# Final stage of a graph-and-experts layer: the weighted sums moved to TensorE as diagonal products

## The reference, cut to what matters

```python
sel = take_along_axis(expert_out, topk_idx)          # two rows of 256 for each node
moe = sum(topk_w[..., None] * sel, axis=2)
y = x + moe                                          # x: the node's own normalised row
mu, var = mean(y), var(y)                            # over the 256 features
out = x_in + (y - mu) / sqrt(var + eps) * gamma + beta
```

## Time and profile before

| | |
|---|---|
| median of three runs | 1391.78 us |
| profiled execution: span from first to last instruction | 1391.8 us |
| mean granted TensorE clock over the span | 0.917 |
| TensorE last busy at | 1314.1 us |
| first load of the final stage issued at | 1317.41 us |
| last VectorE instruction ends at | 1387.63 us |

### The profile page before, as it was taken

One profiled execution on the slowest core, in us unless ns is written; L12 is line 12 of the kernel. 1 busy time (PEld: TensorE's weight loads), 2 busy tenths in 40 slices (PEclk: granted clock), 3 DMA queues, 4 the chain that ended last, 5 costly groups with the idle time before them and its releaser, 6 DMA issues.

```text
span 1391.8 us, 24409 instructions
## 1 busy us (share of the span) xinstructions
PE 1101.7 (79%) x6668; PEld 776.1 (56%) x6669; DVE 910.6 (65%) x2128; ACT 525.3 (38%) x1408; POOL 853.7 (61%) x968
## 2 busy tenths in 40 slices
PE   6799987999968878778887888888943999999700
PEld 4476543444446545545554555557842999999700
DVE  7599998999976666566665666633566333433276
ACT  3567655767713233333333233213420332332212
POOL 5362228999977777777777777750004577755326
PEclk9899998999979999999999999969965999999955
DMA  5000000000023333333333333357722122222392
GB/s 165 16 26 17 14 15 3 0 0 0 0 64 100 103 105 102 102 105 99 106 102 101 104 106 105 104 72 225 256 98 87 61 72 69 71 72 68 83 261 78
DMA packets 50239, 115.99 MB, mean 83 GB/s; under 512 B 11113, under 2 KB 24783, under 8 KB 50040
## 3 DMA queue, kind: packets, MB, share of 16 engines
q0 software_dynamic: 26832, 74.54, 18.6%
q1 hardware_dynamic: 23336, 40.64, 9.7%
HBM read 97.15 MB, written 17.99 MB: 83 GB/s over the span
## 4 chain that ended last, share of the span: by engine, by line
PE 44%; DVE 14%; DMA 14%; issue 13%; POOL 10%; ACT 2%; DVEq 2%; SPq 1%; POOLq 0%; ACTq 0%
PE bank L1813 10%; DMA big<-msg_rows,const 10%; PE bank L2063 8%; PE bank L2074 8%; POOL big L721 5%; POOL big L661 4%; DVE node_buf L1275 3%; PE bank L1757 2%; DVE big L1202 2%; PE bank L1977 2%; PE bank L1774 2%; PE bank L1683 1%; DVE big L1228 1%; DMA big<-xn_rows 1%; DMA x_buf<-x 1%
## 5 line engine op out<-in xcount | busy, mean ns | idle before, releaser
L721 POOL DMA_INDIRECT big<-msg_rows,const x416 | 407.1, 979 | 126.6 <-issue 80.6
L1813 PE MATMUL bank<-big 128*128 128x256 f32 x832 | 242.5, 417 | 88.2 <-DMA big<-msg_rows,const 53.6
L1275 DVE TENSOR_TENSOR node_buf<-node_buf,bank 125x256 f32 x416 | 173.6, 417 | 201.6 <-PE bank L1813 147.7
L1813 PEld LDWEIGHTS bank<-big 128*128 128x128 f32 x832 | 150.7, 201 | 154.2 <-DVE node_buf L1275 88.9
L1202 DVE TENSOR_SCALAR big<-bank,big 125x416 bf16<-125x416 f16 x400 | 183.7, 492 | 0.0
L966 ACT ACTIVATE big<-bank 128x500 f32<-128x500 f32 (+1 forms) x208 | 107.4, 572 | 179.8 <-PE bank L1865 179.8
L1060 ACT ACTIVATE mid<-bank,const 128x128 f32<-128x128 f32 x256 | 73.0, 368 | 207.9 <-PE bank L2063 207.9
L705 POOL TENSOR_TENSOR big<-big 125x512 f32<-125x512 f32 x125 | 142.1, 1172 | 10.6 <-PE bank L1757 9.3
L661 POOL TENSOR_TENSOR big<-big 125x256 f32<-125x256 f32 (+1 forms) x100 | 55.5, 555 | 112.7 <-ACT big L787 106.7
L2074 PE MATMUL bank<-big,mid 128*128 x512 | 121.0, 380 | 0.0
L1683 PE MATMUL bank<-big 125*128 125x416 bf16 x400 | 102.7, 348 | 21.2 <-DVE big L1202 10.2
(11 more groups left out here) (304 smaller groups left out, 2001.5 us busy)
## 6 DMA issues: line engine op xcount, KB each, us to landing
big<-L_ffn_w SPq DMA_DIRECT2D x32, 512.0 KB, 6.1
big<-msg_rows,const POOLq DMA_INDIRECT x416, 2.7
big<-moe_rows SPq DMA_DIRECT2D x10, 560.0 KB
msg_rows<-big SPq DMA_DIRECT2D x25, 125.0 KB
xn_rows<-mid POOLq DMA_DIRECT2D x5, 625.0 KB, 5.9
x_buf<-x SPq DMA_DIRECT2D x5, 560.0 KB
big<-xn_rows SPq DMA_DIRECT2D x5, 560.0 KB
out<-big SPq DMA_DIRECT2D x5, 560.0 KB
```

The costliest lines, as they stand in the source:

```text
L721: pool.indirect_dma_start(msgs[slot], None, msg_rows, bass.IndirectOffsetOnAxis(edge_idx[:, n:n + 1], 0)).then_inc(msgs_in[slot // 2], 16)
L1275: dve.tensor_tensor(rows, rows, agg_ps[2 * half + j][0:P, :], ALU.add).then_inc(s.agg_add, 1)
L1813: mm(agg_ps[k % 4], hot_src[:, turn, k, :], msgs[slot], start=True, stop=True, skip_group_check=True).then_inc(s.agg_mm, 1)
```

## The change

The two weighted sums leave VectorE. Each becomes a product on TensorE with a diagonal matrix: `diag0[t]` is 125 x 125 with the first weights of tile t on its diagonal, `diag1[t]` has the second weights. The own rows are multiplied with the identity, so that three products accumulate own + w0 * pick0 + w1 * pick1 in one PSUM bank (`bank[t % 8]`). VectorE takes the statistics from PSUM, and ScalarE normalises out of PSUM into `pick0`.

- ScalarE makes the diagonals `diag0` (an activation that scales the identity by a column of weights), those of groups 0 and 1 as soon as `y_ok` has reached 64, those of group g + 2 behind the normalising of group g.
- GpSimd makes `diag1` in the same rhythm, behind the `gamma` multiplications of group g, and does no residual additions any more.
- VectorE does all five residual additions of a group, and does those of group g - 1 between the statistics of group g and `shift_of(g)`.
- SP loads the own rows of group 0 when `y_ok` is 64, without waiting for the scatters, and those of group g + 1 behind the expert rows of group g.
- Tile t waits on TensorE for `fin_norm` of tile t - 8, whose bank it takes.

The diff, without the declarations of semaphores and buffers:

```diff
@@ sync engine: loads and stores
+            def load_rows(g, view, dram):
+                rows = slice(G * g, G * g + G)
+                for lo, hi in ((0, 112), (112, P)):
+                    sp.dma_start(view[lo:hi, rows, :], tiled(dram)[lo:hi, rows, :]).then_inc(fin_in[g], 16)
+
+            sp.wait_ge(s.y_ok, NT)
+            load_rows(0, own, xn2_rows)
             for k in range(2):
                 sp.wait_ge(y_out[k], 16 * (NT // 2))
             for g in range(T // G):
-                rows = slice(G * g, G * g + G)
-                for view, dram in ((pick0, moe_rows[0:N]), (pick1, moe_rows[N:2 * N]), (own, xn2_rows)):
-                    for lo, hi in ((0, 112), (112, P)):
-                        sp.dma_start(view[lo:hi, rows, :], tiled(dram)[lo:hi, rows, :]).then_inc(fin_in[g], 16)
+                load_rows(g, pick0, moe_rows[0:N])
+                load_rows(g, pick1, moe_rows[N:2 * N])
+                if g < T // G - 1:
+                    load_rows(g + 1, own, xn2_rows)
             for g in range(T // G):
                 rows = slice(G * g, G * g + G)
-                sp.wait_ge(s.fin_ok, (G - len(VECTOR_ADDS)) * (g + 1))
-                sp.wait_ge(s.fin_ok_too, len(VECTOR_ADDS) * (g + 1))
+                sp.wait_ge(s.fin_ok, G * (g + 1))
@@ GpSimd
-            pool.wait_ge(s.beta_ok, T)
-            for t in range(T):
-                pool.wait_ge(s.fin_norm, t + 1)
-                pool.tensor_tensor(pick0[:, t, :], pick0[:, t, :], gamma_bc, ALU.mult).then_inc(s.fin_gamma, 1)
-                if t % G not in VECTOR_ADDS:
-                    pool.wait_ge(s.fin_gamma, t + 1)
-                    pool.tensor_tensor(pick0[:, t, :], pick0[:, t, :], x_sb[:, t, :], ALU.add).then_inc(s.fin_ok, 1)
+            pool.wait_ge(s.y_ok, NT)
+
+            def second_diagonals(g):
+                for t in range(G * g, G * g + G):
+                    pool.tensor_scalar(diag1[:, t, :], ident[0:P, 0:P], weight[:, t, 1:2], None, ALU.mult).then_inc(s.diag1_ok, 1)
+
+            second_diagonals(0)
+            second_diagonals(1)
+            for g in range(T // G):
+                for t in range(G * g, G * g + G):
+                    pool.wait_ge(s.fin_norm, t + 1)
+                    pool.tensor_tensor(pick0[:, t, :], pick0[:, t, :], gamma_bc, ALU.mult).then_inc(s.fin_gamma, 1)
+                if g + 2 < T // G:
+                    second_diagonals(g + 2)
@@ ScalarE
+            def first_diagonals(g):
+                for t in range(G * g, G * g + G):
+                    act.activation(diag0[:, t, :], ident[0:P, 0:P], ACT.Copy, scale=weight[:, t, 0:1]).then_inc(s.diag0_ok, 1)
+
+            act.wait_ge(s.y_ok, NT)
+            first_diagonals(0)
+            first_diagonals(1)
             for g in range(T // G):
                 act.wait_ge(s.fin_stats, g + 1)
                 act.activation(rstd[:, g * G:g * G + G], mv[:, g * G:g * G + G, 1], ACT.Sqrt, bias=eps_t).then_inc(s.fin_root, 1)
                 act.wait_ge(s.fin_shift, g + 1)
                 for t in range(G * g, G * g + G):
-                    act.activation(pick0[:, t, :], pick1[:, t, :], ACT.Identity, scale=rstd[:, t:t + 1],
+                    act.activation(pick0[:, t, :], bank[t % 8][0:P, 0:D], ACT.Identity, scale=rstd[:, t:t + 1],
                                    bias=fin_shift[:, t:t + 1]).then_inc(s.fin_norm, 1)
+                if g + 2 < T // G:
+                    first_diagonals(g + 2)
@@ VectorE
             def residual(g):
-                for t in [G * g + j for j in VECTOR_ADDS]:
+                for t in range(G * g, G * g + G):
                     dve.wait_ge(s.fin_gamma, t + 1)
-                    dve.tensor_tensor(pick0[:, t, :], pick0[:, t, :], x_sb[:, t, :], ALU.add).then_inc(s.fin_ok_too, 1)
+                    dve.tensor_tensor(pick0[:, t, :], pick0[:, t, :], x_sb[:, t, :], ALU.add).then_inc(s.fin_ok, 1)
             for g in range(T // G):
                 tiles = range(G * g, G * g + G)
-                dve.wait_ge(fin_in[g], 6 * 16)
                 for t in tiles:
-                    last = dve.scalar_tensor_tensor(pick0[:, t, :], pick0[:, t, :], weight[:, t, 0:1], own[:, t, :], ALU.mult, ALU.add)
-                step(last)
-                for t in tiles:
-                    last = dve.scalar_tensor_tensor(pick1[:, t, :], pick1[:, t, :], weight[:, t, 1:2], pick0[:, t, :], ALU.mult, ALU.add)
-                step(last)
-                for t in tiles:
-                    last = dve.bn_stats(stats[:, t, :], pick1[:, t, :])
+                    dve.wait_ge(s.fin_mm, t + 1)
+                    last = dve.bn_stats(stats[:, t, :], bank[t % 8][0:P, 0:D])
                 step(last)
                 for t in tiles:
                     last = dve.bn_aggr(mv[:, t, :], stats[:, t, :])
                 last.then_inc(s.fin_stats, 1)
                 if g:
-                    shift_of(g - 1)
-                if g > 1:
-                    residual(g - 2)
-            shift_of(T // G - 1)
-            residual(T // G - 2)
+                    residual(g - 1)
+                shift_of(g)
             residual(T // G - 1)
@@ TensorE, behind the expert stage
+            pe.wait_ge(s.y_ok, NT)
+            for t in range(T):
+                if t % G == 0:
+                    pe.wait_ge(fin_in[t // G], 6 * 16)
+                if t >= 8:
+                    pe.wait_ge(s.fin_norm, t - 7)
+                total = bank[t % 8][0:P, 0:D]
+                mm(total, ident[0:P, 0:P], own[:, t, :], start=True, stop=False)
+                pe.wait_ge(s.diag0_ok, t + 1)
+                mm(total, diag0[:, t, :], pick0[:, t, :], start=False, stop=False)
+                pe.wait_ge(s.diag1_ok, t + 1)
+                mm(total, diag1[:, t, :], pick1[:, t, :], start=False, stop=True).then_inc(s.fin_mm, 1)
```

More of the change, by code:

```diff
@@ L39 @@
 BEHIND = [[], [], [0, 1], [2, 3], [4]]
-VECTOR_ADDS = (3, 4)
 MAGIC = 12582912.0
@@ L225, in __init__ @@
         self.fin_shift = sem("fin_shift")
+        self.diag0_ok = sem("diag0_ok")
+        self.diag1_ok = sem("diag1_ok")
+        self.fin_mm = sem("fin_mm")
         self.fin_ok = sem("fin_ok")
-        self.fin_ok_too = sem("fin_ok_too")
         self.stored = sem("stored")
@@ L362, in program @@
         own = m.take([T, D], parts=P)
+        diag0 = m.take([T, P], parts=P)
+        diag1 = m.take([T, P], parts=P)
         b = Region(big, 0, NX * 2048)
```

## The result

The changed kernel takes 1376.84 us, the median of four runs (1374.81 to 1378.89), beside 1392.39 for the kernel before (1391.77 to 1394.47, four runs). The ratio is 0.988, with a 95% interval from 0.9864 to 0.9897: 15.6 us less. The forecast was 1376.5, or 15.3 us less.

What follows compares the result with a forecast made beforehand. Loads bound the early groups, then VectorE, slowed beside GpSimd. Group 2's products end at 1347.6; loops of 7.6 us bring group 4's to 1362.8, and the tail of 13.7 gives 1376.5 us, range 1371 to 1387.

Steps and rivals of the forecast that it cites:

- The loads: Start of final stage: own rows of group 0 move while the last scatter lands, so each group lands 2.5 us earlier.
- the case of no gain: Low end for the loads: the early load delays the scatters as much, so the gain is nothing instead of 2.5 us.
- The half clock of group 0: TensorE starts group 0 at half clock: 5 us for two tiles, then 3.9 us for three, 8.9 us in all.
- The loop over the banks: Tile 3 waits for the bank of the previous group's tile 0: 5.0 us plus 2.6 for tiles 3 and 4, 7.6 a group.
- the waits at tile 3: Sign expected in the changed profile: TensorE's waits inside a group fall on the normalising, at tile 3.
- The tail: From group 4's last product to the end: 5.0, multiplications 4.0, last addition 0.5, and 4.2 to the end: 13.7 us.
- Contention: Final stage before: two-input VectorE work beside two-input GpSimd work takes 0.79 us an instruction, not 0.41; 10.65 us a group.
- the rival of no gain: VectorE and GpSimd stay at 10.65 us a group for another reason; kernel about 1390 us; chance 0.04.
- GpSimd's diagonals: Making diagonals on GpSimd: 0.28 to 0.60 us each, nearest 0.41; a GpSimd group of multiplications and diagonals 6.1 us.
- Statistics from PSUM: VectorE statistics read from PSUM: no difference taken from SBUF; 0.1 us either way a piece, at most 0.5 us a group.
- half-clock case: Rivals on TensorE: half clock throughout, 1402 us, chance 0.08; or at the start of every group, 1383 us, chance 0.10.
- Stores ahead of the loads: Rival: early stores make groups 3 and 4 land 2.5 and 5 us later; kernel 1379 to 1381 us; chance 0.10.

Runs made afterwards that it cites:

- first experiment: Changed kernel with group 0's own rows loaded behind the wait for the scatters, ahead of the expert rows: ratio to the kernel before 0.9909, 63.4 us of stage.
- third experiment: Changed kernel with 28 unused products on TensorE before the first landing to keep the clock up: ratio to the kernel before 0.9908, 63.2 us of stage.
- the quiet GpSimd: Kernel before, GpSimd silent in the final stage: gamma multiplications left out, all residual additions and the sums on VectorE; ratio 0.9891, 62.5 us of stage.

## Why the prediction was right, step by step

**The time** was right by luck in part, since errors cancelled. The forecast sum, counted into the stage, is 47.9 us to the last product and 13.7 to the end, 61.6. Measured: 49.5 and 12.3, 61.8. Behind the 49.5 is a second pair of errors: TensorE began 2.8 us later than forecast and took 0.5 us more for group 0, and then won back 1.7 us over groups 2 to 4, which took 21.1 us and not three times 7.6. What was right without luck: VectorE no longer bounds the stage, its sums no longer collide with GpSimd, and TensorE keeps up.

**The loads**: wrong. I let the own rows of group 0 move "while the last scatter lands" for nothing and took the full 2.5 us. The first group came 12.5 us into the stage, not 9.7, and the last 42.8, not 38.6. The first experiment shows that the early load made the scatter late. I had named the case of no gain as one end, and chose the other. Part of the rest of the 4.2 us may be in how I read the end of the loads before: I took 1356, but from 1355.8 to 1358.3 the transfer engines still had a share of 0.54 with 217 GB/s, part of it the first store.

**The half clock of group 0**: right in size. It held for 5.6 us (5 taken) and group 0 was done 9.4 us after its start (8.9). But my sum carried it on to the end: without it the same sum has group 1 end at 1338.7 and not at 1340.0, and the kernel 0.8 us sooner. The third experiment shows that nothing of it reaches the end, since the later groups wait for their loads.

**The loop over the banks**: its size was wrong, and with it the bound. I took 5.0 us from the last product of a group to its first normalised tile, with additions of 0.60 between ends of 0.42 and 0.79. The 0.42 is the duration of one record; in a row they take 0.33, and 0.36 beside the diagonals. So from the last product of group 1 (done at 1340.24) to the first normalised tile (1343.83) it was 3.6 us, below even my short end of 4.1. TensorE asks for that bank after three tiles, 3.9 us, so the waits at tile 3 that I had named as a sign did not come, but for 0.15 us in all. In place of this loop the loads set the later groups: 7.2 to 8.4 us a group in the third experiment, against the 7.6 that I had from the other cause. The equal numbers hid that. That it was the loads is shown by the five landings of the third experiment, and by what the shift placed first did not bring. The margin is small, though: group 4 of the changed kernel found TensorE only 0.24 us idle.

**The tail**: 12.3 for 13.7. The five additions of group 3, 1.65 us in place of 3.0, are 1.35 of the 1.4 us. The five multiplications took 4.00 us, as forecast, and what follows them 4.7, as forecast.

**Contention**: the reason that I gave for 10.65 us a group, two-input work on both engines at once, was right, and the quiet GpSimd shows it: 9.0 of the 10.8 us by which the last shift came earlier are to be had by silence there alone. With it falls the rival of no gain: the 10.65 us a group had no other reason. I did not see what follows, that the sums need not leave VectorE to be fast, if its neighbour's two-input work does; whether a complete kernel gets there that way is not shown.

**GpSimd's diagonals**: 0.58 us alone (ten in 5.81), 0.68 on average, above the 0.60 that I gave as the long end. A round of GpSimd, five multiplications and five diagonals, was 6.9 to 7.2 us in place of 6.1, close to the pace of the loads. It did not matter with groups of five, where TensorE waited for no diagonal; it did with smaller ones.

**Statistics from PSUM**: 15 ns more than from SBUF. From the fixed cycles of the Trainium skill (VectorE: DVE Perf Modes, section on the TRN2 errata), 120 for PSUM and 58 for SBUF, the estimate was about 65 ns; the measurement decides.

**The rivals**: the clock came up after 5.6 us and stayed up through pauses of 1.3 us, and of 1.6 us in the third experiment, so neither half-clock case came. The HAM oscillation of the Trainium skill (TensorE: Matmul & The Clock Gate, section on HAM oscillation) is not seen in these traces. Its example has longer waits for transfers than these, so this does not speak against the page, but against taking it over to pauses this short. Stores ahead of the loads: refuted for an effect of 5 us.

Open are the spread of the load times from run to run (the last landing from 42.5 to 44.2 us into the stage with the same order of transfers), what exactly the early load is worth at the end, and what a complete kernel with the sums on VectorE and no two-input work on GpSimd beside them would take.

## What to carry to other kernels

Before moving work to another engine, look whether the engine is slow or only disturbed: the same instruction in an early group, with its neighbour idle, and in a late one tells it at once, 0.41 against 0.79 us here. After such a change a transfer is soon the bound, and then only what follows the last landing counts. Smaller groups at the end, together with the shift first, the clock kept up and all diagonals ahead, brought 5.6 us of stage. No run has the smaller groups alone, but the shift first brought 0.5 us behind the last product, since the additions collided again, and the clock kept up brought nothing. A load that is issued early into idle-looking transfer engines is not free if it shares them with the transfer on which the next step waits.

## What the runs showed of the hardware that I had not expected

- A load of 640 KB issued 0.25 us ahead of the last scatter moved the step that waits for the scatter from 2.5 to 5.0 us after its issue (4.5 to 5.3 in eleven traces), about the time of the load itself.
- Two-input work on VectorE and GpSimd collides wherever it meets: an addition beside a multiplication has a record of 0.94 us, one with GpSimd idle 0.42. Beside GpSimd's diagonals, with one input each, five additions took 1.82 us in place of 1.73.
- Multiplying a 125 x 125 matrix with a column of numbers takes 0.58 us on GpSimd and 0.30 on ScalarE, in the same stretch of the same kernel.
